# A selective-scan sequence loop on one core: softplus' end moved to GpSimd, reversed sums over a pair, 16 products with C on VectorE, and y summed by fp32 transposes

## The reference, cut to what matters

```python
def _selective_scan(u, dt, A, B, C, D, reverse=False):
    dA = jnp.einsum('bld,dn->bldn', dt, A)
    dB_u = jnp.einsum('bld,bld,bln->bldn', dt, u, B)
    if reverse: dA = jnp.flip(dA, 1); dB_u = jnp.flip(dB_u, 1)
    dA_shift = jnp.pad(dA[:, 1:], ((0, 0), (0, 1), (0, 0), (0, 0)))
    dA_cum = jnp.exp(jnp.flip(jnp.cumsum(jnp.flip(dA_shift, 1), 1), 1))
    xs = jnp.cumsum(dB_u * dA_cum, 1) / (dA_cum + 1e-12)
    y = jnp.einsum('bldn,bln->bld', xs, C)
    if reverse: y = jnp.flip(y, 1)
    return y + u * D
# per direction: delta, B, C = split(x @ x_proj_w.T)
#                delta = softplus(delta @ dt_proj_w.T + dt_proj_b)
#                y = _selective_scan(...) * silu(res)
# x = layernorm(x + (y + y_b) @ out_proj_w.T)
# x = layernorm(x + soft_moe(layernorm(x)))
```

## Time and profile before

| what | value |
|---|---|
| median of 3 runs | 6359.67 us (6358.49 to 6361.42) |
| the profiled execution, its own time | 6359.75 us |
| its span in the profile | 6357.9 us |
| mean granted TensorE clock | 0.922 |
| busy over the span: PE, DVE, ACT, POOL | 5209.8, 4991.7, 4293.1, 4827.9 us |
| instructions: PE, DVE, ACT, POOL | 14632, 4307, 6696, 2327 |

### The profile page before, as it was taken

The page is one execution under the profiler, slowest core; times in us unless marked ns, Lnnn a source line. Parts: engine busy times, 40 slices in busy tenths (PEclk is TensorE's granted clock), DMA queues, the critical chain, the costliest instruction groups (busy, mean ns, idle before and its releaser), DMA issues. The chain is left out here.

```text
span 6357.9 us, 71115 instructions
## 1 busy us (share of the span) xinstructions
PE 5209.8 (82%) x14632; PEld 2567.4 (40%) x14632; DVE 4991.7 (79%) x4307; ACT 4293.1 (68%) x6696; POOL 4827.9 (76%) x2327
## 2 busy tenths in 40 slices
PE   6878888878788888887887878887878787999977
PEld 2333333333333333333333333333333334555566
DVE  6998989898989898989899999899999892222233
ACT  4878787778778787787877878787878783111100
POOL 3999999899999999898989999999999991000000
PEclk8999899999999999899989989898989898999988
DMA  2444343333333333343443333333333332322265
GB/s 72 124 116 124 118 125 118 122 118 123 116 122 119 124 117 124 114 125 114 126 114 120 119 118 120 123 120 118 117 120 115 124 115 78 96 87 84 75 220 210
DMA packets 555713, 755.58 MB, mean 119 GB/s; under 512 B 124059, under 2 KB 272411, under 8 KB 553245
## 3 DMA queue, kind: packets, MB, share of 16 engines
q1 hardware_dynamic: 555293, 752.04, 38.0%
HBM read 662.04 MB, written 89.82 MB: 118 GB/s over the span
## 5 line engine op out<-in xcount | busy, mean ns | idle before, releaser
L640 POOL TENSOR_TENSOR g_ring<-dtu,b_ring 128x1024 f32<-128x1024 f32 x1026 | 2478.8, 2420 | 209.2 <-DVE e_ps L1008 160.3
L1008 DVE TENSOR_TENSOR_SCAN e_ps<-e_ps,g_ring 128x1024 f32<-128x1024 f32 x1024 | 2344.2, 2289 | 157.6 <-ACT e_ps L804 122.4
L1173 PE MATMUL y_ps<-v_ring,ident 128*128 128x512 f32 x3596 | 1939.1, 647 | 475.8 <-POOL v_ring L649 434.7
L649 POOL TENSOR_TENSOR v_ring<-z_ring,c_ring 128x1024 f32<-128x1024 f32 x896 | 2216.9, 2475 | 55.7 <-PE y_ps L1173 55.4
L804 ACT ACTIVATE e_ps<-dt,a_neg 128x512 f32<-128x512 f32 x2050 | 1398.1, 682 | 633.6 <-DVE z_ring L1021 381.8
L814 ACT ACTIVATE f_ring<-rsum,consts,a_neg_half 128x512 f32<-128x512 f32 x2050 | 1648.1, 804 | 0.9
L1021 DVE SCALAR_TENSOR_TENSOR z_ring<-f_ring,e_ps 128x1024 f32<-128x1024 f32 x896 | 1090.4, 1217 | 144.6 <-DVE e_ps L1008 92.0
L1173 PEld LDWEIGHTS y_ps<-v_ring,ident 128*128 128x128 f32 x3596 | 668.1, 203 | 1324.5 <-issue 672.7
L1106 PE MATMUL side<-u,conv_diag 128*128 128x512 f32 x1088 | 505.7, 609 | 65.8 <-ACT disp_ring L765 61.3
L1283 ACT ACTIVATE x_act<-x_gate,x_bg 128x512 f32<-128x512 f32 x128 | 87.9, 687 | 562.6 <-PE x_gate L1315 562.6
L1143 PE MATMUL side<-xnT,seT 128*128 128x512 f32 x544 | 301.5, 684 | 143.8 <-ACT sT_ring L743 143.8
(11 more groups left out here) (135 smaller groups left out, 5704.2 us busy)
## 6 DMA issues: line engine op xcount, KB each, us to landing
b_ring<-bc_scr SPq DMA_DIRECT2D x1027, 256.0 KB, 3.4
c_ring<-bc_scr SPq DMA_DIRECT2D x1025, 256.0 KB, 3.3
pT_scr<-rowT_ring SPq DMA_DIRECT2D x136, 256.0 KB, 3.6
m_pT<-pT_scr SPq DMA_DIRECT2D x16, 2048.0 KB, 8.3
sT_scr<-sT_ring SPq DMA_DIRECT2D x272, 64.0 KB, 2.5
x_xT<-sT_scr SPq DMA_DIRECT2D x16, 1024.0 KB, 8.8
eo_scr<-x_eo SPq DMA_DIRECT2D x32, 512.0 KB, 5.1
m_eo<-eo_scr SPq DMA_DIRECT2D x16, 1024.0 KB, 10.8
```

The lines of the kernel that those rows point to most:

```text
L640: pool.tensor_tensor(g_ring[:, k], dtu[d][:], both(b_ring[:, k:k + 1]), ALU.mult).then_inc(g_done, 1)
L649: pool.tensor_tensor(v_ring[:, k], z_ring[:, k], both(c_ring[:, k:k + 1]), ALU.mult).then_inc(v_pool, 1)
L1008: dve.tensor_tensor_scan(e, e, g, 0.0, ALU.mult, ALU.add).then_inc(scan_done, 1)
L1173: pe.matmul(y_ps[:, t % 2], ident[:], v, start=(t % (TILES // PAIRS) < 2), stop=True, skip_group_check=True).then_inc(v_used, 1)
```

## The change

Four things are changed together, all in `sequence_stage`.

Softplus: the "1 +" is undone by a new ACT instruction (`less_done`, lag 5), the correction is a plain subtraction on POOL (`softplus_fix`, lag 6), the last subtraction and the product with u are two pair-wide POOL instructions (`softplus_end`, lag 8).

Reversed sums: one scan over the 1023 elements of a pair in place of two over 511. A row `border` of ones with a zero in the middle stops the sum between the chunks.

Products with C: `ON_DVE` holds every fourth step, 16 per sequence, and `v_own` has two buffers.

y: `add_state` turns each 128x128 block of v with a transpose that accumulates in PSUM, so `y_ps` has positions on the partitions. The gate `res` is computed in that layout (the operands of its matmul are exchanged), the skip term too, and before the output projection four new slots `yT0` to `yT3` transpose the gated y back, with ACT copying it to `ygT`. The table of slots is shifted accordingly.

```diff
-        dt1_0 dt1_1 out0 out1 res0 res1 res2 res3 xnT0 xnT1
+        dt1_0 dt1_1 yT0 yT1 out0 yT2 yT3 out1 res0 res1 res2 res3 xnT0 xnT1
...
-STATS_TILE, VAR_TILE, ROUGH_TILE, RSTD_TILE, APPLY_TILE = 15, 18, 20, 22, 25
+STATS_TILE, VAR_TILE, ROUGH_TILE, RSTD_TILE, APPLY_TILE = 20, 23, 25, 27, 30
...
+    FIX_LAG, DT_LAG, RSUM_LAG, CUT_LAG = 6, 8, 10, 12
-    ON_DVE = [i for i in range(STEPS) if i % 8 == 4]
+    ON_DVE = [i for i in range(STEPS) if i % 4 == 1]
...
-        v_own = sb("v_own", [P, 2, L])
+        v_own = sb("v_own", [P, 2, 2, L])
+        border = sb("border", [P, 2 * L - 1])
...  on POOL
-            def dtu_of_chunk(at, s, i):
+            def softplus_fix(at, s):
+                d = int(TABLE[s][0][-1])
+                pool.wait_ge(less_done, at.pair(s))
+                for j in (s - 1, s):
+                    pool.wait_ge(side_free[at.bank(j)], at.freed(j))
+                pool.tensor_tensor(sp_exp[d][:], sp_exp[d][:], dt[d][:], ALU.subtract).then_inc(fix_done, 1)
+            def softplus_end(at, s):
+                d, i = int(TABLE[s][0][-1]), TABLE[s][1]
+                pool.wait_ge(ln_done, at.pair(s))
+                pool.wait_ge(fix_done, at.pair(s))
+                pool.tensor_tensor(dt[d][:], sp_one[d][:], sp_exp[d][:], ALU.subtract).then_inc(dt_done, 1)
                 pool.wait_ge(dt_done, at.pair(s))
-                pool.tensor_tensor(dtu[d][:, i % 2], dt[d][:, i % 2], u[d][:, i, PAD:], ALU.mult).then_inc(dtu_done, 1)
+                pool.tensor_tensor(dtu[d][:], dt[d][:], u[d][:, i - 1:i + 1, PAD:], ALU.mult).then_inc(dtu_done, 1)
...  on ACT
+                    elif kind == "yT":
+                        act.activation(ygT[:, i % 2], src.rearrange("p (c l) -> p c l", c=KI), ACT.Copy).then_inc(free, 1)
...
+                        act.activation(sp_exp[d][:], sp_one[d][:], ACT.Identity, bias=less_one).then_inc(less_done, 1)
...  on DVE
-                        dve.scalar_tensor_tensor(out=sp_exp[d][:], in0=sp_one[d][:], scalar=1.0,
-                                                 in1=dt[d][:], op0=ALU.subtract, op1=ALU.subtract).then_inc(fix_done, 1)
...
-                        dve.tensor_tensor(dt[d][:], sp_one[d][:], sp_exp[d][:],
-                                          ALU.subtract).then_inc(dt_done, 1)
...
-                        dve.tensor_tensor_scan(out, one.broadcast_to([P, L - 1]), data, 0.0,
-                                               ALU.mult, ALU.add).then_inc(rsum_done, 1)
+                        dve.tensor_tensor_scan(out, data, turn, 0.0, ALU.add, ALU.mult).then_inc(rsum_done, 1)
...  on PE
-                pe.matmul(y_ps[:, t % 2], ident[:], v, start=(t % (TILES // PAIRS) < 2),
-                          stop=True, skip_group_check=True).then_inc(v_used, 1)
+                for lb in range(LT):
+                    mm = pe.matmul(rows_of(lb, t % 2), v[:, lb * P:(lb + 1) * P], ident[:], is_transpose=True,
+                                   start=(t % (TILES // PAIRS) == 0 and lb % 2 == 0), stop=True, skip_group_check=True)
+                mm.then_inc(v_used, 1)
```

More of the change, by code:

```diff
@@ L159 @@
     ("x0", 0), ("x1", 0), ("dt0", 0), ("dt0", 1))
-EPILOGUE = ("out", "xnT", "rows", "cols", "rowsT", "colsT", "slots")
+EPILOGUE = ("yT", "out", "xnT", "rows", "cols", "rowsT", "colsT", "slots")
 def sequence_stage(nc, xT, x, in_wT, conv_w, conv_b, x_wT, dt_wT, A_log, D, out_wT,
@@ L663, in _ @@
                 if TABLE[s] == ("dt0", 1):
-                    for i in range(2):
-                        dtu_of_chunk(pro, s, i)
+                    softplus_fix(pro, s)
+                    softplus_end(pro, s)
+                    cut_chunks(pro, s)
             for gi in range(G_AHEAD):
@@ L818, in _ @@
             for s in PRO:
-                for lag in range(2, 10):
+                for lag in range(2, 13):
                     side_step(pro, s, lag)
@@ L984, in y_gate @@
             def y_gate(at, b, p):
-                for i in (2 * p, 2 * p + 1):
+                for i in (2, 3):
                     s = TABLE.index(("res", i))
@@ L1091, in fill @@
                 pe.wait_ge(side_free[at.bank(s)], at.freed(s, 0))
-                if kind in ("in0", "res"):
-                    if kind == "in0" and i == 0:
+                if kind == "in0":
+                    if i == 0:
                         pe.wait_ge(xT_loaded, at.seq(s) * 16 + 16)
-                    m = i if kind == "in0" else KI + i
                     for k in range(KM):
-                        mm = pe.matmul(bank, w_in[:, k, m * P:(m + 1) * P], xT_t[:, k], start=(k == 0), stop=(k == KM - 1))
+                        mm = pe.matmul(bank, w_in[:, k, i * P:(i + 1) * P], xT_t[:, k], start=(k == 0), stop=(k == KM - 1))
+                elif kind == "res":
+                    for k in range(KM):
+                        mm = pe.matmul(bank, xT_t[:, k, i * P:(i + 1) * P], w_in[:, k, DI:2 * DI],
+                                       start=(k == 0), stop=(k == KM - 1))
+                elif kind == "yT":
+                    if i == 0:
+                        pe.wait_ge(y_gated, at.seq(s) * 2 + 1)
+                    for c in range(KI):
+                        mm = pe.transpose(bank[:, c * P:(c + 1) * P], yg[:, i, c * P:(c + 1) * P], ident[:])
                 elif kind in ("conv0", "conv1"):
@@ L1183, in _ @@
                     for d, q, pair in SKIPS.get(turn, ()):
-                        pe.matmul(y_ps[:, q], d_diag[:, d, 2 * pair + q], u[d][:, 2 * pair + q, PAD:],
-                                  start=False, stop=True, skip_group_check=True)
+                        for lb in range(LT):
+                            pe.matmul(rows_of(lb, q), u[d][:, 2 * pair + q, PAD + lb * P:PAD + (lb + 1) * P],
+                                      d_diag[:, d, 2 * pair + q], start=False, stop=True, skip_group_check=True)
                     for s in range(SLOTS):
```

88 lines of the change are left out of this document (47 added, 41 removed).

## The result

The changed kernel took 6285.02 us (median of 4 runs, 6277.07 to 6295.57) against 6359.08 us. The ratio is 0.9889, with a 95% interval of 0.9866 to 0.9912. Timed again on another chip it was 0.9907 [0.9889, 0.9926]. So it is faster by 1.1%. The forecast was 6160, 3.1% faster: the direction is right, the gain is about a third of what was forecast. The time lies just inside the range of 6090 to 6290, where the prediction had put rival (a), not its own sum.

The account below looks back on a forecast made before the run. DVE's path (318.4 us per sequence) was taken as the bound, POOL's 309 close behind; they fall to 304.2 and 304.6, plus 5 coupling: 309.5. Saving 210 over 16 sequences, adding 8 outside, gives 6160 us; range 6090 to 6290.

Parts of the forecast that it names:

- rival (a): Waits stay on POOL, idling 21 us as before because the longer softplus chain hands stalls on; 6322 us; chance 0.19.
- the busy times: Sequence loop, busy per sequence: DVE from 291.6 to 278.9 us, POOL from 301.2 to 298.3.
- The sum's mean: Reversed sum of 1023 elements on DVE: 2.3 us free plus a wait of 1.5, so 3.8 each, 15.2 per sequence.
- PE's work: y by four transposes saves PE 54 us over 128 tiles, leaving 186 us per sequence at the full clock.
- the two 1.5: PE frees v and the gate sooner, taking 1.5 us per sequence off both DVE's and POOL's idle time.
- a coupling of 5: Two nearly equal paths, DVE and POOL, make the loop take 5 us per sequence more than the longer one.
- 25.3: DVE's idle time not owed to POOL, per sequence: down from 26.8 to 25.3 us.
- POOL's wait for PE: POOL idle for PE, 47.2 us in 14 sequences, falls by 1.5 per sequence; PE's standing at out1 stays hidden.
- The wait for ACT's decay: DVE waiting for ACT, 7.8 us per sequence: 2.5 off for the norm chain's spacing, 2 added for new ACT work.
- The wait for the output projection: PE would stand some microseconds at out1 for ACT's copy, hidden by POOL's three v buffers; no DVE wait was counted.
- signs of being wrong: Wrong if y additions release POOL in most sequences, the sum's mean exceeds 6 us, or decay holds DVE over 12.
- rival (b): TensorE's clock falls to the lower level with less work; about 6950 us if PE sets the pace throughout; slower, chance 0.09.

Follow-up runs that it names:

- e4: Changed kernel with 8 products with C on VectorE, every eighth step, in place of 16 per sequence; 6410.48 us, ratio 1.0121.
- e5: Kernel before with softplus' end on GpSimd and the pair-wide sum alone, 8 products with C on VectorE, old y; 6332.46 us, ratio 0.9994.
- e1: Changed kernel with y as before: one matmul per tile, old gate layout, no yT slots, old table; 6187.46 us, ratio 0.977.
- e9: Changed kernel with dt0_2 at tile 38 (was 34), VectorE taking up the output projection a tile later, norm two tiles later; 6221.13 us, ratio 0.98.
- e10: Changed kernel without yT slots and their copies, table of before; output projection reads gated y directly, so its result isn't the reference's; 6132.08 us, ratio 0.9661.
- e7: e1 with the norm's five tiles as late as in the changed kernel; 6256.13 us, ratio 0.9849.
- e6: Changed kernel with two matmuls of zeros added into y_ps after each tile's four transposes; 6339.55 us, ratio 0.9975.
- e11: e1 with a hold of 7 in place of 5 for the dt slots in the table; 6113.86 us, ratio 0.9633.

## Why the prediction was wrong, step by step

**Right: the busy times.** DVE was to go to 278.9 us per sequence and went to 278.2, POOL to 298.3 and went to 298.3. The sum's mean was 3.38 us (3.8 taken), free 2.28 (2.3), and it lengthens a GpSimd instruction by 2.0 us (2.1). The norm's wait of 4.8 us at step 11 went. The wait at the reversed sum is gone. e4 and e5 confirm POOL's path from the other side: with 8 products more it is busy 316.5 to 316.8 us (317), and then it is the bound. PE's work was sized right too: 224.7 busy at a granted 0.81 is 183 us at the full clock (186 taken); only that it would be busy "near 200" missed, because the clock fell further. The additions, half as long at the full clock, went from 136 to 83 us of PE's busy time per sequence.

**Near, and partly by luck: the sum for the kernel without y's part.** Without the two 1.5 that y was to give back, the prediction has two paths of about 306 and a coupling of 5 (what two equal paths cost one another), so 311, and e1 took 311.8. But two errors cancel in it. DVE's idle time not owed to POOL is 34.7 us in e1 (26.8 by the prediction without y's 1.5), and DVE waits only 0.2 us for POOL, so that the 5 for coupling is not there.

**Wrong: the idle time.** The step that failed is "25.3" for DVE's idle time not owed to POOL, and with it POOL's wait for PE, 3.4 us (47.2/14) of which 1.5 were to go. They came out at 40.1 and 12.8. Three terms were mis-sized:

- The wait for ACT's decay was to be 7.8 - 2.5 + 2 = 7.3 and is 20.6. 5.9 of it is at step 21, behind the late projection `in0_0`, and 2.5 each at steps 38 and 54, behind the logarithm. In e1 it is 15.0, so the larger part of the miss is not y's. What the waits at steps 38 and 54 cost was not tested: no run takes them out.
- The wait for the output projection was put at nothing and is 6.1. It is gone in e9, and 2.5 us per sequence with it.
- POOL's wait for PE: the text said that PE's standing at `out1` is hidden "as long as POOL's three v buffers last" and took 1.5 us off twice, since PE has less to do. PE does have less to do (224.7 us busy against 260.7), but most of its wait is not for its own work. PE goes through its instructions in order, so a slot whose bank or input is late holds the y additions, and through `v_used` POOL, and through the slot's copy ACT and DVE's decay. I priced what a slot computes, not the tile at which it stands against the tile at which what it needs is there. These tiles stand in the code: 36 + 4 for the dt bank against 38 for in0_0, 9 + 2 for the copy against 11 for `out0`. In e1 the wait is 9.4 already. At step 47 (2.9 us, 3.7 in e1) it is of another kind: there PE runs its slots without a gap, and the y additions come after them.

Two of the prediction's own signs of being wrong came true: PE's y additions hold up POOL in every sequence, and ACT's decay holds up DVE for more than 12 us. Rival (a), that POOL idles 21 us as before, came near in time (319.7 per sequence against 318.4) and in idle time (20.1), but not for its reason: 12.8 of the idle time waits for PE, and the longer softplus chain shows no stall of POOL in e5 and none in e1. The chances beside the range don't fit one another either: 0.13 lies above 6347, so "about 0.14 above" 6290 leaves 0.01 for 6290 to 6347, where (a), with 0.19, has its own time of 6322.

Of the 1.2% of y's part between e1 and the changed kernel: the transposes give 1.1% (e10 against e1), so slots and table take 2.3%. Of these the late norm alone takes 0.8% (e7 against e1). Taking the squeeze apart and giving the projection a tile more brings back 0.9% (e9). The remaining 1.4% between e9 and e10 were not separated: four more slots, their copies on ACT, and a norm seven tiles later than in e10 go together there. e1, e7 and e10 ran on three chips, and each number is a difference of ratios with intervals of 0.2 to 0.4% to either side.

**The clock, rival (b).** It fell to 0.81 in the loop and nearly doubled single instructions (the 6.62 us of `in0`, against 3.67), but it isn't what set the time: e10 is fast at 0.82, e7 has the late norm's loss at 0.92, and e6 raised the clock and lost. What the low clock costs on top, in the 6.62 us for one, no run separates. On the rule of the Trainium skill, page "TensorE: Matmul & The Clock Gate", section "Part 4: PE-mode transpose", that transposes don't count as PE being busy in the same way: no run here separates that from PE simply having less to do and idling more, so it stays open.

## What to carry to other kernels

In a loop with a written order, sum the busy times for the floor, then check each moved or added slot's tile against the tile at which its buffer and inputs are ready: an engine with spare time that works in order passes such a wait on to those that have none. When a change shifts one anchor of a table and leaves the next, look at what is squeezed between them. A relief of the two fullest engines can make an order matter that did not matter before, as the hold of e11 shows: worth nothing in the old kernel, 1.4% on e1, and a loss on e9. It can also lay open waits that their own work had filled, as behind the logarithm here.

## What the runs showed of the hardware

An fp32 matmul of 512 columns against the identity takes two records of 0.43 us (two take 1.02 with the last one's tail); the same 128x512 block by four accumulating fp32 transposes takes four of 0.11 (four take 0.60 with the tail, at 2436.66 above), half the time, at the full clock. A DVE instruction that reads two SBUF inputs beside a busy GpSimd may lose several turns (10.40 us for 1.22 of work), while the sum of 1023 elements, at 2.28 us free, never took over 4.45.
